# Expert 0's tokens picked with one-hot products on the chip, in place of a scatter and a load

## The reference, cut to what matters

```
x = x + relu(segment_sum(norm * h[row], col))        # 1250 nodes of 512 features
xt = layernorm(x)
logits = xt @ Wr + br                                # 8 experts
probs = softmax(logits); G = max(probs); idx = argmax(probs)
h1 = relu(xt @ W1[idx] + b1[idx])                    # 512 -> 512
y = G * (h1 @ W2[idx] + b2[idx])                     # 512 -> 512
out = x + y
```

## Time and profile before

| | us |
|---|---|
| median of 3 runs | 577.86 (577.47 to 579.46) |
| the profiled execution | 577.9 |
| its span, first to last instruction | 576.1 |
| mean granted TensorE clock | 0.962 |
| TensorE busy | 506.1 (88%) |
| VectorE busy | 463.3 (80%) |
| ScalarE busy | 330.2 (57%) |
| GpSimd busy | 71.9 (12%) |

### The profile page before, as it was taken

The page is one execution under the profiler, slowest core; times in us unless marked ns, Lnnn a source line. Parts: engine busy times, 40 slices in busy tenths (PEclk is TensorE's granted clock), DMA queues, the critical chain, the costliest instruction groups (busy, mean ns, idle before and its releaser), DMA issues.

```text
span 576.1 us, 11968 instructions
## 1 busy us (share of the span) xinstructions
PE 506.1 (88%) x4587; PEld 375.0 (65%) x4588; DVE 463.3 (80%) x911; ACT 330.2 (57%) x645; POOL 71.9 (12%) x83
## 2 busy tenths in 40 slices
PE   1889999887589999999899799979999857999995
PEld 1777777666588888887777544434566627667762
DVE  7989999799899999995889658995656626787681
ACT  5355555567789999984765523345221318766730
POOL 3000000000000000000000200223243320222342
PEclk9959999999899999999999889999999977999999
DMA  7970000002011111100000094000011159266111
GB/s 184 358 257 2 1 2 1 2 12 85 2 47 48 48 48 47 48 3 1 1 1 2 33 317 180 1 0 3 2 41 55 57 182 381 75 216 230 59 52 51
DMA packets 25306, 45.14 MB, mean 78 GB/s; under 512 B 6961, under 2 KB 7205, under 8 KB 25248
## 3 DMA queue, kind: packets, MB, share of 16 engines
q1 hardware_dynamic: 23264, 39.16, 19.8%
q0 software_dynamic: 1952, 5.18, 2.5%
q10 hardware_dynamic: 32, 0.01, 0.0%
HBM read 33.23 MB, written 11.95 MB: 78 GB/s over the span
## 4 chain that ended last, share of the span: by engine, by line
PE 47%; DVE 32%; issue 12%; POOL 3%; ACT 3%; DMA 2%; ACTq 0%; POOLq 0%; DVEq 0%
PE bank L1704 8%; PE bank L1350 7%; PE bank L1692 6%; PE bank L1417 5%; PE bank L1374 4%; DVE work L1064 4%; DVE big L932 4%; PE bank L1424 4%; PE bank L1521 3%; PE bank L1534 2%; PE bank L1328 2%; DVE rings L1064 2%; POOL row L482 2%; DVE st L831 1%; DVE work L969 1%
## 5 line engine op out<-in xcount | busy, mean ns | idle before, releaser
L932 DVE TENSOR_TENSOR big<-mid 128x1536 f16<-128x1536 f16 (+1 forms) x100 | 92.0, 978 | 0.0
L1417 PE MATMUL bank<-big 128*128 128x160 f16 x552 | 75.3, 255 | 4.1 <-DVE big L932 4.1
L1521 PE MATMUL bank<-big,work 128*128 128x130 f16 x1080 | 67.5, 225 | 8.4 <-DVE work L1064 8.4
L1521 PEld LDWEIGHTS bank<-big,work 128*128 128x128 f16 x1080 | 64.3, 100 | 10.4 <-DVE work L1064 4.9
L1417 PEld LDWEIGHTS bank<-big 128*128 128x128 f16 x552 | 54.3, 115 | 7.1 <-DVE big L932 6.3
L650 ACT ACTIVATE mid<-aux,small 128x1280 f16<-128x1280 f32 x36 | 47.4, 1350 | 0.7 <-DVE work L1064 0.4
L1534 PE MATMUL bank<-big,mid 128*128 128x260 f16 x400 | 47.1, 275 | 0.1
L1614 PE MATMUL bank<-mid 128*128 128x512 f16 x200 | 45.9, 379 | 0.0
L549 ACT ACTIVATE big<-bank 128x160 f32 x92 | 27.8, 303 | 28.2 <-PE bank L1424 26.9
L1534 PEld LDWEIGHTS bank<-big,mid 128*128 128x128 f16 x400 | 38.2, 96 | 7.5 <-issue 0.3
L549 ACT ACTIVATE mid<-bank 128x160 f32 x92 | 27.7, 301 | 26.5 <-PE bank L1424 25.1
(11 more groups left out here) (300 smaller groups left out, 1099.8 us busy)
## 6 DMA issues: line engine op xcount, KB each, us to landing
big<-in_L_ffn_W SPq DMA_DIRECT2D x10, 1024.0 KB, 9.2
mid<-in_L_ffn_W SPq DMA_DIRECT2D x6, 1024.0 KB, 14.3
xperm_scratch<-work SPq DMA_DIRECT2D x1, 5753.0 KB, 20.7
aux<-thr_scratch SPq DMA_DIRECT2D x8, 640.0 KB, 3.7
aux<-xperm_scratch SPq DMA_DIRECT2D x8, 523.0 KB, 3.6
row<-in_x SPq DMA_DIRECT2D x1, 2304.0 KB
aux<-in_L_gnn_Ws SPq DMA_DIRECT2D x4, 256.0 KB, 4.3
work<-in_L_gnn_W SPq DMA_DIRECT2D x1, 1024.0 KB, 14.3
```

The lines of the kernel that those rows point to most:

```text
L932: return V.tensor_tensor(out.rearrange("p c (v two) -> p c v two", two=2), values.rearrange("p (v two) -> p v two", two=2).unsqueeze(1).to ...
L1417: mm(count_bank(base, k)[:, 0:RW], L_ring[:, slot, k * CH + j, :], R_ring[:, slot, k * CH + j, :], start=j == 0, stop=False)
L1521: ins = mm(acc_region(h, t), weighted[i % NC][:, t * P:(t + 1) * P], VP[:, s, part, h, :, :].rearrange("p b f -> p (b f)"), start=False, s ...
```

## The change

While a tile's LayerNorm values are at hand, ScalarE normalizes its rows twice (`token_rows`): to float32 and to the 16-bit high half `token16[:, t, 0]`. VectorE makes the low half (`token_low`). In `place`, VectorE also writes a one-hot `sel` of 128 tokens by 208 slots: slot equal to rank, times "the expert is 0". TensorE multiplies the halves by `sel` (`pick`: eight products of 208 columns for a tile), and the sum over the ten tiles in banks 6 and 7 is expert 0's normalized tokens, already transposed. So `rows(0)` and `token_T(0)` are gone. All rows, those of expert 0 too, are still scattered, and expert 0's slot is still loaded for its gate, its numbers and its residual. `token16` lies in the same memory as the slots `xs`, so the loads now wait for the picks as well (`xs_psum`).

The order changes around it. `ranks(t)` follows `lin_d(t)` in the same turn, `stay_warm` and the 24 products of zeros go, the transposition of `b1` moves to an earlier stage, with its copy going from ScalarE to VectorE. `m1(0)` becomes `m1_first`, which takes the two halves of the features as they come. The second block of `m2(0)` stands behind `token_T(1)`, and `token_T(2)` and `m1(1)` follow it. On ScalarE `w_hi(1, 0)`, `hidden(0)` and `w_hi(1, 1)`, on VectorE `h_split(0)` and `split_w(1, 1)`, come ahead of what needs loaded tokens.

```diff
+            nc.gpsimd.iota(slots, [[1, S1]], base=0, **kw)
             nc.gpsimd.memset(b2_nat, 0.0).then_inc(sem("b2_zeroed"), 1)
...
             sp.wait_ge(sem("scattered"), 16 * T)
+            sp.wait_ge(sem("xs_psum"), 2)
...
+            def token_rows(t):
+                a.wait_ge(sem("ln_rs"), 3 * T + t + 1)
+                if t >= 2:
+                    a.wait_ge(sem("token_lo"), t - 1)
+                for dst in (xh_ring[:, t % 2, :], token16[:, t, 0, :]):
+                    ins = act(dst, x[:, t, :], ACT.Identity, bias=row[:, t, D:D + 1], scale=row[:, t, D + 1:D + 2])
+                ins.then_inc(sem("token_hi"), 1)
...
+            for t in range(T - 1):
                 rows_copy(t)
...
+                if t + 2 < T:
                     ln_sqrt(3 * T + t + 1)
+                    token_rows(t)
                     relu(t + 2)
+            token_rows(T - 2)
+            rows_copy(T - 1)
+            ln_sqrt(4 * T - 1)
+            token_rows(T - 1)
...
-            rows(0)
             x_hi(0)
+            w_hi(1, 0)
+            hidden(0)
+            w_hi(1, 1)
             rows(1)
-            gates(0)
-            gates(1)
-            w_hi(1, 1)
-            hidden(0)
             x_hi(1)
+            rows(2)
             w_hi(2, 0)
-            rows(2)
-            gates(2)
+            for e in range(3):
+                gates(e)
...
+                V.tensor_scalar(sel[:, t, :], slots, rank[:, t:t + 1], oh[:, t, 0:1], ALU.is_equal, ALU.mult).then_inc(sem("sel_made"), 1)
...
+            def token_low(t):
+                v.wait_ge(sem("token_hi"), t + 1)
+                V.tensor_tensor(token16[:, t, 1, :], xh_ring[:, t % 2, :], token16[:, t, 0, :], ALU.subtract).then_inc(sem("token_lo"), 1)
...
+            for t in range(T):
+                v.wait_ge(sem("x4_made"), t + 1)
+                ln_stats(3 * T + t, x[:, t, :], row[:, t, D:D + 2])
                 if t >= 1:
                     logits(t - 1)
+                row_offsets(t)
+                if t >= 1:
+                    place(t - 1)
+                if 1 <= t < T - 1:
+                    token_low(t - 1)
+            logits(T - 1)
+            token_low(T - 2)
+            token_low(T - 1)
             place(T - 1)
...
+            x_lo(0)
             v.wait_ge(sem("total_psum"), 1)
...
-            x_lo(0)
+            h_split(0)
+            split_w(1, 1)
             names(0)
             names(1)
-            split_w(1, 1)
-            h_split(0)
             x_lo(1)
...
+            def pick(t, q):
+                pe.wait_ge(sem("token_lo"), t + 1)
+                pe.wait_ge(sem("sel_made"), t + 1)
+                for kk in range(2):
+                    k = 2 * q + kk
+                    for part in range(2):
+                        ins = mm(bank[6 + q][:, kk * S1:(kk + 1) * S1], token16[:, t, part, k * P:(k + 1) * P], sel[:, t, :],
+                                 start=False, stop=t == T - 1 and kk == 1 and part == 1)
+                return ins
...
+            for t in range(T - 2):
                 rows_T(t)
+                agg(t + 2, 0, 5)
                 lin_d(t)
+                agg(t + 2, 5, 9)
+                ranks(t)
+                agg(t + 2, 9, T)
+            rows_T(T - 2)
+            pe.wait_ge(sem("relu_made"), T)
+            for q in range(2):
+                mm(bank[6 + q][:, 0:2 * S1], zero16[:, 0:P], zero16[:, :], start=True, stop=False)
+            pick_both(0)
+            lin_d(T - 2)
+            rows_T(T - 1)
+            pick_both(1)
+            lin_d(T - 1)
+            pick_both(2)
+            ranks(T - 2)
+            pick_both(3)
+            pick_both(4)
             ranks(T - 1)
...
+            for t in range(5, T - 2):
+                pick_both(t)
+            for q in range(2):
+                pick(T - 2, q)
+                pick(T - 1, q).then_inc(sem("xs_psum"), 1)
...
+            m1_first()
+            pe.wait_ge(sem("b2_lo"), 1)
+            m2(0, (0,))
             pe.wait_ge(sem("te_ready"), 1)
-            token_T(0)
-            m1(0)
             token_T(1)
-            for e in range(E1):
+            m2(0, (1,))
+            token_T(2)
+            m1(1)
+            for e in range(1, E1):
```

More of the change, by code:

```diff
@@ L48 @@
 FILL_A = 24
-FILL_G = 5
 BY_ACT = (0, 1, 2, 3, 4, 6, 7, 8, 9)
@@ L63 @@
 EPS = 1e-5
-FILL_H = 24
 SLOPE = 0.2
@@ L125, in gnn_ffn_kernel @@
         iota16 = sb("iota16", [P, E0])
-        small = sb("small", [P, 1536])
+        small = sb("small", [P, 1408])
         mid = sb("mid", [P, E1 * K * D])
@@ L202, in gnn_ffn_kernel @@
         rtmp, o = carve(work, o, [2, D])
+        sel, o = carve(work, 2 * 2 * D, [T, S1], F16)
+        slots, o = carve(work, o, [S1], F16)
         sum_junk = hs[:, 0, :].rearrange("p (k m) -> p k m", k=K)
@@ L1605, in _, with agg @@
             pe.wait_ge(sem("ff_used"), T)
-            def agg(t, half):
-                if t >= 2 and half == 0:
+            def agg(t, s0, s1):
+                if t >= 2 and s0 == 0:
                     pe.wait_ge(sem("relu_made"), t - 1)
-                for s in range(half * T // 2, (half + 1) * T // 2):
+                for s in range(s0, s1):
                     if t == 0:
@@ L1615, in agg @@
                                  start=s == 0 and part == 0, stop=s == T - 1 and part == 1)
-                if half:
+                if s1 == T:
                     ins.then_inc(sem("agg_done"), 1)
@@ L1640, in rows_T @@
                 transposes(x[:, t, :], bank[t % 2], "xt_psum")
-            def stay_warm():
-                for _ in range(FILL_G):
-                    mm(bank[6][:, 0:400], zero16[:, 0:P], zero16[:, :], start=True, stop=True)
-            for t in range(2):
-                agg(t, 0)
-                agg(t, 1)
-            for t in range(T):
-                rows_T(t)
-                if t + 2 < T:
-                    agg(t + 2, 0)
-                else:
-                    pe.wait_ge(sem("relu_made"), T - 1)
-                    stay_warm()
-                lin_d(t)
-                if t:
-                    ranks(t - 1)
-                if t + 2 < T:
-                    agg(t + 2, 1)
+            def pick(t, q):
[7 more added lines that the diff above has]
+                return ins
@@ new lines, in pick_both @@
+            def pick_both(t):
+                pick(t, 0)
+                pick(t, 1)
+            agg(0, 0, T)
+            agg(1, 0, T)
+            for t in range(T - 2):
+                rows_T(t)
+                agg(t + 2, 0, 5)
+                lin_d(t)
+                agg(t + 2, 5, 9)
[5 more added lines that the diff above has]
+                mm(bank[6 + q][:, 0:2 * S1], zero16[:, 0:P], zero16[:, :], start=True, stop=False)
@@ L1669, in token_T @@
+            for t in range(5, T - 2):
+                pick_both(t)
+            for q in range(2):
+                pick(T - 2, q)
+                pick(T - 1, q).then_inc(sem("xs_psum"), 1)
             def token_T(e):
-                pe.wait_ge(sem("xs_normed"), 2 * (e + 1))
+                pe.wait_ge(sem("xs_normed"), 2 * e)
                 for q in range(2):
-                    if e:
-                        pe.wait_ge(sem("x_lo"), 2 * (e - 1) + q + 1)
+                    pe.wait_ge(sem("x_lo"), 2 * (e - 1) + q + 1)
@@ L1694, in m1, with m1_first, m2 @@
                     ins.then_inc(sem("m1_done"), 1)
-            def m2(e):
+            def m1_first():
+                pe.wait_ge(sem("w_lo0"), 1)
+                for q in range(2):
+                    mm(bank[2 + q][:, 0:2 * S1], zero16[:, 0:P], zero16[:, :], start=True, stop=False)
+                for xq in range(2):
+                    pe.wait_ge(sem("x_lo"), xq + 1)
+                    for f in range(K):
+                        for k in (2 * xq, 2 * xq + 1):
+                            for n, (wp, xp) in enumerate(PARTS):
+                                ins = mm(bank[2 + f // 2][:, f % 2 * S1:(f % 2 + 1) * S1], W16[0][0][:, wp, k, f * P:(f + 1) * P],
+                                         xT16[:, 0, xp, k, :], start=False, stop=k == K - 1 and f % 2 == 1 and n == 2)
+                        if xq and f % 2:
+                            ins.then_inc(sem("m1_done"), 1)
+            def m2(e, blocks=(0, 1)):
                 pe.wait_ge(sem("w_lo1"), e + 1)
-                pe.wait_ge(sem("h_lo16"), 2 * e + 2)
                 if e >= 2:
                     pe.wait_ge(sem("res_made"), 2 * (e - 1))
-                for j, m in enumerate((P, S1 - P)):
+                for j in blocks:
+                    m = (P, S1 - P)[j]
                     mm(bank[4 + 2 * (e % 2) + j][0:m, :], pick16[:, e:e + 1].to_broadcast([64, m]), b2_16, start=True, stop=False)
                     for n, (k, (wp, hp_)) in enumerate((k, c) for k in range(K) for c in PARTS):
+                        if n % (K // 2 * len(PARTS)) == 0:
+                            pe.wait_ge(sem("h_lo16"), 2 * e + k // 2 + 1)
```

63 lines of the change are left out of this document (21 added, 42 removed).

## The result

| | before | after |
|---|---|---|
| median of 12 runs, us | 577.66 (575.7 to 579.7) | 572.56 (569.56 to 577.16) |
| profiled execution, span | 577.9, 576.1 | 573.0, 571.2 |
| aggregation's last tile, A | 452.29 | 453.54 |
| end of expert 0's first layer, M | 483.31 | 471.84 |
| end of expert 1's first layer, E | 490.71 | 485.99 |

The ratio after to before is 0.9923, 95% interval 0.9901 to 0.9945: faster by 5.1 us by the medians and 4.4 by the ratio, where 4.3 were forecast. Terms of the sum were wrong with opposite signs.

A forecast was written before the change was run, and what follows sets the result against it. It took the TensorE-paced aggregation, then expert 0's trip through DRAM, as the bound. A 455.9, plus 18.05, 13.1 and 61.5, put expert 7 at 548.6, 4.3 us gained: 577.9 - 4.3 = 573.6 us, range 569.5 to 577.5.

The forecast's parts named there:

- What bounds it now: Aggregation runs at TensorE's pace; then 31.0 us pass until expert 0's first layer ends, while TensorE mostly waits.
- A: End of the aggregation: moves from 452.29 to about 455.9, by 0.45, 0.5, 0.3 and 2.4 us.
- The eight stalls of 0.3: Aggregation tiles: `token_low` waits beside GpSimd's residual add, delaying the one-hot; 0.3 us a tile, 2.4 for eight.
- A to M: From the aggregation's end through the picks to the end of expert 0's first layer: 18.05 us, M at 473.95.
- M to E: From the end of expert 0's first layer to that of expert 1's: 13.1 us, E at 487.05; part is given back.
- I take it as just hidden: Expert 1's token load lands at A + 21.85, ScalarE wants it at A + 20.8; costed at nothing, other bound 1.05.
- The rival in which the trip changes its owner: Expert 1 waits for scatter and load instead of expert 0: E 1.05 to 2 later, 574.6 to 575.6; chance 0.09.
- E to the end: From expert 1's first layer to the start of expert 7's: E + 61.5, set by the token slots, start at 548.6.
- The clock: Rival: it falls while the picks wait, so expert 0's 48 products take twice 4.28; 577.9, no change; chance 0.14.
- the ring: Expert rounds: reused token slots (result, put, load, names, next result) now set the end, 12.0 us a round against TensorE's 11.11.
- The loop through ScalarE: Slower rival: relu, add, `token_low`, statistics and normalizations bind the aggregation; at 7.1 us a tile, 580; chance 0.1.
- More is gained: Rival: `token_low` and the add miss each other, 571.2 or 570.4; with shorter slot rounds too, about 569; chance 0.22.

The follow-up runs named there:

- low_first: The kernel after, with VectorE making the low half of a tile's tokens ahead of `place` instead of behind it: median 572.33 us, ratio to before 0.9915.
- m2_behind: The kernel after, with TensorE's order behind expert 0's first layer again token_T(1), m1(1), token_T(2), m2(0): median 571.10 us, ratio to before 0.9917.
- no_ring: The kernel after, with own slots for the tokens of experts 4 to 7, loaded without waiting for a put: median 569.28 us, ratio to before 0.9852.
- split_later: The kernel after, with VectorE's split of second-layer weights behind result(e) moved one turn later: median 569.82 us, ratio to before 0.9844.
- no_ring_early: no_ring plus expert 1's tokens loaded first, tile 5 picked ahead of the last ranks, 14 zero products behind m1(1): median 566.36 us, ratio to before 0.9803.
- names_behind: The kernel after, with names(e + 3) behind result(e) on VectorE, so result(e) no longer waits for that load: median 570.60 us, ratio to before 0.9888.

## Why the prediction was right, step by step

**What bounds it now.** Right: the stretch from A to M fell from 31.02 to 18.30. That is 12.7, of which 6.7 is given back between M and E (7.40 before, 14.15 after); the rest is the gain.

**A.** The mis-sized term. Forecast + 3.65, measured + 1.25, and 0.47 of that lies ahead of the first tile (404.25 and 404.72). From the first tile to A it is 48.04 before, 48.82 and 48.79 in the two profiles after, so about + 0.8 belongs to the change; 5.90 gained behind A less 0.8 is the 5.1 of the medians. The first tile took 0.74 more, of which TensorE's wait for the one-hot is 0.34 (0.95 forecast with the rank pair). The iota cost nothing (0.3 forecast): it took 0.32, and GpSimd stood idle for 3.38 before the first add. The eight stalls of 0.3, 2.4 in all, came to 0.4, and even that was paid for by a tile that is 0.06 shorter without them (5.98 on average before, 5.92 in low_first). The mechanism of the earlier trace rows was there, on the other side: `token_low` came 0.07 ahead of the add instead of within it, so the add was late, by 0.47, and not VectorE by 1.2. The one-hot ended 5.09 after the tile's first transpose where 5.45 had been worked out and TensorE wanted it at 5.12.

**A to M.** Right: 18.05 forecast, 18.30 measured, with the ranks at A + 8.91 (8.75) and the first products at A + 13.85 (13.75). The 18.30 came back in every kernel that left this part alone.

**M to E.** Forecast 13.1, measured 14.15. The other bound came true: the load let ScalarE start at A + 21.84, against the 21.85 worked out from the earlier trace rows, while ScalarE wanted it at A + 20.90. "I take it as just hidden" was the step that failed in this execution. It holds in others: low_first and m2_behind did not wait, and low_first has 13.09 from M to E. The rival in which the trip changes its owner was part of the truth, by 0 to 1.36.

**E to the end.** Right: 61.55 forecast, 62.11 measured, result(0) 7.51 after E, rows(4) 9.99 later, the three rounds 35.64, the rest 8.97. What the prediction had as a fixed length, 12.0 a round, held a stall of 1.9 in each of these puts, in the kernel before as well; no_ring and split_later showed TensorE's own way behind it, and no_ring_early its 58.30, against 58.4 forecast for TensorE alone.

**The rivals.** The clock did not fall while the picks waited (1.00 from 461 to 462); it fell in expert 2's first layer, where the ring hid it. The loop through ScalarE did not bind. "More is gained" was true of the stall and not of the ring. So 2.4 too much at A stood against 0.25, 1.05 and 0.56 too little behind it: 548.6 forecast for expert 7, 548.10 measured. One start was misread as well: 552.91 for expert 7 in the kernel before is from the chain, and the timeline, from which the other starts come, has 552.75; so TensorE's rounds were 11.08 and not 11.11, and the gain at that point was 4.65. The number was right, and better than its terms: that is luck.

## What to carry to other kernels

When a stall is removed, work out the next loop that comes due (here slot, result, put, load) with its length from the trace, and then ask what is inside that length: an issue that takes three times as long beside one other instruction is a price of the order, not of the transfer. Give a rule about a shared port to every pair of neighbours on the two engines, not only to the one that the change adds. A gain counts only ahead of what sets the end: the same products of zeros were worth nothing with the ring, and with it gone no_ring_early got all that its edits were worked out to bring.

## What was not expected of the hardware

- The second half of a put takes 0.92, and 2.86 when a split of 128x2048 on VectorE starts 0.23 ahead of it; it then ends 0.80 after the split (profile of after, four times).
- Which engine gives way can't be told from the recorded starts here: `token_low`, recorded 0.07 ahead of the add, kept its 0.68 and the add went from 1.26 to 1.73 (after); `sel`, recorded 0.08 ahead of the add, went from 0.33 to 1.42 and the add kept 1.26 (low_first).
- A first layer behind 2.93 without TensorE work took 6.10 instead of 4.44, at a granted clock of 0.56 in its first 3 us, that is mostly the lower of the two levels. The same gap does not always do it: behind the 2.93 of names_behind the layer took 4.44. Behind 1.57 in the kernel after the clock stayed; behind 1.99 in split_later and 4.25 in m2_behind it fell.
